# Merge blocks requested first in their slot, weight parts and constants moved in the prologue, one more float32 score tile

## The reference, cut to what matters

```python
# x: (8, 512, 512); ctx: (8, 77, 512); 16 experts, head size 64
def xattn(v, k, q, mask, W_merge, b_merge):
    scores = where(mask, -1e9, einsum('bqd,bkd->bqk', q, k) / sqrt(512))
    atted = einsum('bqk,bkd->bqd', softmax(scores), v)
    return einsum('bdl,ol->bdo', swapaxes(atted, -1, -2), W_merge) + b_merge
x = x + xattn(ctx, ctx, layernorm(x), mask, W_merge, b_merge)

h = layernorm(x).reshape(4, 1024, 512)
logits = l2norm(h) @ l2norm(sim_matrix) - sigmoid(gates)
rw = softmax over the open experts of relu(logits)       # two best ones if none is open
q, k, v = [sum over e of rw[..., e] * (h @ proj[e]) for proj in (q_proj, k_proj, v_proj)]
attn = causal softmax(q k' / 8) v
x = x + sum over e of (rw[..., e] * attn) @ o_proj[e]
```

## Time and profile before

| what | value |
|---|---|
| time before, median of 3 runs | 899.1 us (898.63 to 899.4) |
| the profiled execution, its own time | 897.96 us |
| its span | 896.2 us |
| its mean granted TensorE clock | 0.992 |
| PE busy | 871.1 us, 97% of the span |
| DVE / ACT / POOL busy | 71% / 25% / 14% |
| DMA | 96.96 MB, mean 108 GB/s |

### The profile page before, as it was taken

The page is one execution under the profiler, slowest core; times in us unless marked ns, Lnnn a source line. Parts: engine busy times, 40 slices in busy tenths (PEclk is TensorE's granted clock), DMA queues, the critical chain, the costliest instruction groups (busy, mean ns, idle before and its releaser), DMA issues.

```text
span 896.2 us, 15900 instructions
## 1 busy us (share of the span) xinstructions
PE 871.1 (97%) x4872; PEld 814.1 (91%) x4872; DVE 637.3 (71%) x1946; ACT 225.0 (25%) x567; POOL 127.2 (14%) x335
## 2 busy tenths in 40 slices
PE   6689999999999999999999999999999999999998
PEld 5689999999999999999999999999999999999996
DVE  6888868777586786767768577775767667576674
ACT  5522322213131222213212132221322112121131
POOL 5121111211011110111102011110111201011100
PEclk9799999999999999999999999999999999999999
DMA  9736415054141531425214351224415152131302
GB/s 320 288 121 167 151 51 142 27 154 129 49 132 39 164 107 61 120 59 176 84 62 120 99 166 53 86 84 130 150 38 148 35 136 92 35 98 36 97 25 94
DMA packets 68194, 96.96 MB, mean 108 GB/s; under 512 B 10905, under 2 KB 34105, under 8 KB 67874
## 3 DMA queue, kind: packets, MB, share of 16 engines
q1 hardware_dynamic: 59106, 86.79, 31.6%
q10 hardware_dynamic: 9024, 9.44, 4.5%
HBM read 77.07 MB, written 19.14 MB: 107 GB/s over the span
## 4 chain that ended last, share of the span: by engine, by line
issue 68%; PE 16%; POOLq 10%; POOL 3%; DMA 1%; DVE 1%; SPq 0%; DVEq 0%; ACT 0%; ACTq 0%
PE psQ L1328 9%; POOLq L616 2%; POOLq L596 2%; POOLq L619 2%; PE psM L1429 2%; PE psO L1429 2%; PE psQ L1429 1%; POOL limit L599 1%; POOLq L598 1%; POOLq L613 1%; POOLq L621 1%; POOL pow_out L622 1%; POOL pow_tmp L612 1%; DMA MASK<-in_mask 1%; DMA merge_lo<-merge_scratch 0%
## 5 line engine op out<-in xcount | busy, mean ns | idle before, releaser
L1328 PE MATMUL psQ<-Wqkv_hi,hT_hi 128*128 128x384 f32 (+1 forms) x1024 | 351.7, 343 | 1.8 <-DVE hT_lo L893 1.4
L1328 PE MATMUL psQ<-Wqkv_hi,hT_lo 128*128 128x384 f32 (+1 forms) x1024 | 347.3, 339 | 0.0
L1328 PE MATMUL psQ<-Wqkv_lo,hT_hi 128*128 128x384 f32 (+1 forms) x1024 | 347.2, 339 | 0.0
L1030 DVE SCALAR_TENSOR_TENSOR acc<-psQ,RW,acc 128x192 f32<-128x192 f32 x448 | 164.7, 411 | 116.5 <-PE psQ L1328 114.3
L1328 PEld LDWEIGHTS psQ<-Wqkv_hi,hT_hi 128*128 128x128 f32 x1024 | 193.7, 189 | 8.1 <-DVE hT_lo L893 1.8
L1328 PEld LDWEIGHTS psQ<-Wqkv_lo,hT_hi 128*128 128x128 f32 x1024 | 193.9, 189 | 4.6
L1328 PEld LDWEIGHTS psQ<-Wqkv_hi,hT_lo 128*128 128x128 f32 x1024 | 193.3, 189 | 0.0
L611 POOL TENSOR_TENSOR pow_tmp<-b_mv,eps 128x1 f32<-128x1 f32 x32 | 8.1, 254 | 670.5 <-DVE b_mv L983 670.5
L849 ACT ACTIVATE mixedT_hi<-spread 128x512 fp32r<-128x512 f32 x64 | 40.5, 632 | 189.2 <-DVE spread L1204 144.1
L1429 PE MATMUL psO<-Wo_hi,mixedT_hi 128*128 128x512 f32 x120 | 51.6, 430 | 0.2 <-DVE mixedT_lo L1192 0.2
L1429 PE MATMUL psO<-Wo_hi,mixedT_lo 128*128 128x512 f32 x120 | 47.2, 393 | 0.0
(11 more groups left out here) (206 smaller groups left out, 1305.3 us busy)
## 6 DMA issues: line engine op xcount, KB each, us to landing
X<-in_x SPq DMA_DIRECT2D x32, 256.0 KB, 2.7
x_scratch<-X SPq DMA_DIRECT2D x32, 256.0 KB, 2.0
spread<-gates_scratch ACTq DMA_DIRECT2D x16, 512.0 KB, 6.9
resid<-x_scratch SPq DMA_DIRECT2D x32, 256.0 KB, 4.4
out<-resid SPq DMA_DIRECT2D x32, 256.0 KB, 2.4
merge_hi<-merge_scratch SPq DMA_DIRECT2D x28, 256.0 KB, 2.9
merge_lo<-merge_scratch SPq DMA_DIRECT2D x28, 256.0 KB, 3.5
spread<-gates_scratch SPq DMA_DIRECT2D x14, 512.0 KB, 6.8
```

Of the source, the lines that this page charges most:

```text
L1030: dve.scalar_tensor_tensor(out=acc[e][:], in0=src, scalar=w, in1=acc[e][:], op0=ALU.mult, op1=ALU.add).then_inc(expert_added, 1)
L1328: last = pe.matmul(psQ[g % 4][:, 0:first_col(g) + PW], a[:, c * P:(c + 1) * P], w[:, c, E + g * PW - first_col(g):E + (g + 1) * PW], start ...
```

## The change

Six edits. `load_merge` moves to an earlier place in SP's slot, right behind the loads hung on bank turns. The tile with index 5 (the sixth) gets its context scores in float32 (`WHOLE = 6`): `turned_high` and `turned_low` drop out for it, `x1_whole_score` reads the transposed tile from `XT[1]`, and `x1_limit` takes its short form. On ACT all eight `w_high` stand in the prologue, parts 3 and 4 ahead of `copy_rows(0)`. On DVE the chain for `neg_sig` and the scaling of `sim_f` change places, `w_low(0, 0)` stands ahead of `add_x2`, `w_low(0, 1)` ahead of `normalise`, `w_low(1)` ahead of `low_rows(0)`. On POOL the power for `sim_rn` comes one turn of its loop later.

```diff
-W_AHEAD = 6
+WHOLE = 6
+        def is_whole(t1):
+            return isinstance(t1, int) and t1 < WHOLE
...
 # SP, in the slot
                             if work == "h" and cross and live(t + X1_LEAD + 1, N_TILES):
                                 load_x1(t + X1_LEAD + 1, (j + 2) % TILES, n)
+                        if qkv and k in G_AT:
+                            n = TILES * b + G_AT[k] + 1
+                            if live(n, N_TILES - TILES):
+                                load_merge(n, (G_AT[k] + 1) % TILES)
                         if prepare and g == SUM_SLOT + 1:
                             keep_x2(t + 1)
...
                             store_gates(b, GATES_T_AT[k - 1], gates_moved)
-                        if qkv and k in G_AT:
-                            n = TILES * b + G_AT[k] + 1
-                            if live(n, N_TILES - TILES):
-                                load_merge(n, (G_AT[k] + 1) % TILES)
 # POOL, prologue
-                    if n == 2:
+                    if n == TILES - 1:
                         pool.wait_ge(sim_floored, 1)
                         pool.tensor_tensor(sim_rn, sim_ss, half_e, ALU.pow).then_inc(sim_rooted, 1)
 # ACT, prologue
-                w_high(1)
-                w_high(2)
+                for g in range(1, 5):
+                    w_high(g)
                 copy_rows(0)
+                w_high(5)
+                w_high(6)
                 slice_high(1)
-                for g in range(3, W_AHEAD):
-                    w_high(g)
+                w_high(7)
 # ACT, in the slot
-                        if qkv and is_first(b) and k + W_AHEAD < PAIRS:
-                            w_high(k + W_AHEAD)
-                        if cross and g == X1_HIGH_SLOT:
+                        if cross and g == X1_HIGH_SLOT and not is_whole(t1):
                             turned_high(t1, p1)
 # DVE, prologue
                 x1_low(3, 3, 1)
+                dve.wait_ge(gate_e_made, 1)
+                link(dve.tensor_scalar(gate_e, gate_e, 1.0, None, ALU.add))
+                link(dve.reciprocal(gate_e, gate_e))
+                link(dve.tensor_scalar(neg_sig[:], gate_e, -1.0, None, ALU.mult))
+                low_ctx()
+                slice_low(0)
+                dve.wait_ge(ld_x[TILES], 32)
+                x1_moments(TILES, 0, x_first[TILES])
                 dve.wait_ge(sim_rooted, 1)
                 for c in range(KC):
                     last = dve.tensor_tensor(sim_f[:, c, :], sim_f[:, c, :], sim_rn, ALU.mult)
                 last.then_inc(sim_normed, 1)
-                low_ctx()
-                slice_low(0)
-                dve.wait_ge(ld_x[TILES], 32)
-                x1_moments(TILES, 0, x_first[TILES])
                 G_low(0)
+                w_low(0, 0)
                 x2_moved = add_x2(None)
                 row_stats(x2_moved)
-                w_low(0, 0)
                 dve.wait_ge(sim_hi, 1)
                 dve.tensor_tensor(simn[1], sim_f, simn[0].bitcast(F32), ALU.subtract).then_inc(sim_lo, 1)
+                w_low(0, 1)
                 normalise(0, 0)
-                w_low(0, 1)
+                w_low(1)
                 low_rows(0)
-                w_low(1)
-                dve.wait_ge(gate_e_made, 1)
-                link(dve.tensor_scalar(gate_e, gate_e, 1.0, None, ALU.add))
-                link(dve.reciprocal(gate_e, gate_e))
-                link(dve.tensor_scalar(neg_sig[:], gate_e, -1.0, None, ALU.mult))
                 w_low(2)
+                w_low(3)
                 slice_low(1)
-                w_low(3)
 # DVE, in the slot; x1_limit and turned_low take is_whole / WHOLE in the same way
-                        if cross and g == X1_HIGH_SLOT:
+                        if cross and g == X1_HIGH_SLOT and not is_whole(t1):
                             turned_low(t1, p1)
 # PE
                 def x1_whole_score(n):
-                    bank = next_bank(ld_xt[n], 16, has_high=False)
+                    if n < X1_LEAD:
+                        bank = next_bank(ld_xt[n], 16, has_high=False)
+                        tile = xt_first[n]
+                    else:
+                        bank = next_bank(xt_in, 16 * (n - X1_LEAD + 1), has_high=False)
+                        tile = XT[1][:]
...
                         if cross and g == X1_SCORE_SLOT:
-                            x1_score(t + X1_LEAD, (j + 1) % 2)
+                            if is_whole(t + X1_LEAD):
+                                x1_whole_score(t + X1_LEAD)
+                            else:
+                                x1_score(t + X1_LEAD, (j + 1) % 2)
```

More of the change, by code:

```diff
@@ L898, in turned_low @@
                 def turned_low(t1, p):
-                    dve.wait_ge(xt_hi, t1 - X1_LEAD + 1)
+                    dve.wait_ge(xt_hi, t1 - WHOLE + 1)
                     dve.tensor_tensor(hT[p][1][:], XT[p][:], hT[p][0][:].bitcast(F32), ALU.subtract).then_inc(xt_lo, 1)
@@ L920, in x1_limit @@
                     bank = psT[moves.bank()]
-                    if isinstance(t1, int) and t1 < X1_LEAD:
+                    if is_whole(t1):
                         dve.wait_ge(x1_scale_ready, t1 + 1)
@@ L1249, in x1_score @@
                 def x1_score(t1, p):
-                    bank = next_bank(xt_lo, t1 - X1_LEAD + 1, has_high=False)
+                    bank = next_bank(xt_lo, t1 - WHOLE + 1, has_high=False)
                     for c in range(KC):
@@ L1267, in x1_whole_score @@
                     for c in range(KC):
-                        last = pe.matmul(bank[:, 0:C], xt_first[n][:, c * P:(c + 1) * P], ctx_f[n // TILES][:, c, 0:C],
+                        last = pe.matmul(bank[:, 0:C], tile[:, c * P:(c + 1) * P], ctx_f[n // TILES][:, c, 0:C],
                                          start=(c == 0), stop=(c == KC - 1))
```

## The result

The changed kernel takes 893.03 us in the median of 6 runs (890.68 to 893.72), the one before 898.98 in the median of 6 (898.07 to 899.4). The ratio is 0.9932, with a 95% interval from 0.9919 to 0.9945: faster by 6 us or 0.7%. Forecast were 893.9 and a range from 891.3 to 896.5.

A forecast was written before the change was run, and what follows sets the result against it. TensorE bounds the kernel, waiting for merge blocks and, in the first batch, for DVE. Merge -3.8, DVE's list less the late start -2.8, clock +1.4 make -5.2: median 899.1 becomes 893.9 us, range 891.3 to 896.5.

The forecast's parts named there:

- The merge blocks: TensorE's waits for merge second halves: six of seven go with SP's earlier load, -3.8 us, bounds 2.5 and 4.2.
- the slower rival: `ctx_raw`, queued behind 512 KB of merge, lands late and ACT waits; at about 7 us landing 903.5 us; chance 0.03.
- DVE's list: First batch: 3.0 us leaves DVE's work between the first rows' split and the second tile's `normalise`; 2.8 net of late start.
- ACT's two moved parts: `w_high(3)` and `(4)` in ACT's prologue, 1.5 us each, fill 3.0 of its idle 3.75.
- The removed part of `x1_limit`: Two operations leave DVE's list in the first batch, only lengthening its 0.46 us wait for POOL's limit.
- The start: Prologue up to G comes 0.2 us late, bounds -0.3 and 0.8; inserted parts behind it have cover.
- the 0.9: `w_low(0, 1)` ahead of the first `normalise` can hold up POOL's `powers(0)`, making the start up to 0.9 us worse.
- The clock: One 2.5 us TensorE wait ahead of the second tile's transposes, then the clock falls: +1.4 us, from 0 to 1.7.
- The chances given, 0.47 to 0.25: The forecast with the clock's fall, 893.9 us, chance 0.47, against the rival without the fall, 892.5 us, chance 0.25.

The follow-up runs named there:

- e1: The kernel before with only SP's new order, `load_merge` moved earlier; 894.51 us against 898.03, 0.9964.
- e7: The changed kernel with `w_low(1)` back behind `low_rows(0)`; 893.55 us against 898.48 for the kernel before, 0.9948.
- e12: The changed kernel with 12 unread filler matmuls in TensorE's wait and the sixth tile's scores from halves; 891.56 us against 898.42 for the kernel before, 0.9922.
- e3: The changed kernel with the sixth tile's context scores made of halves again; 892.23 us against 898.03 for the kernel before, 0.9944.
- e10: The changed kernel timed again, unedited, on another run's chip; 893.16 us against 898.42 for the kernel before, 0.9944.
- e6: The changed kernel with 12 unread matmuls in TensorE's wait for the second tile's rows; 891.93 us against 898.48 for the kernel before, 0.9928.
- e4: The changed kernel with the second tile's `normalise` ahead of `x1_limit` and `w_low(7)` behind it; 890.93 us against 898.03 for the kernel before, 0.9921.
- e5: The changed kernel with the fifth tile's `x1_moments` and the scaling of `sim_f` behind `G_low(0)`; 891.71 us against 898.48 for the kernel before, 0.9930.
- e8: The changed kernel with only the scaling of `sim_f` put behind `G_low`; 892.76 us against 898.48 for the kernel before, 0.9927.
- e11: The changed kernel with 12 unread filler matmuls, timed again on the unedited changed kernel's chip; 892.04 us against 898.42 for the kernel before, 0.9926.
- e2: The changed kernel with `load_merge` back behind `store_gates`; 896.05 us against 898.03 for the kernel before, 0.9969.
- e9: The changed kernel with e4's and e5's edits together; 891.1 us against 898.42 for the kernel before, 0.9914.

## Why the prediction was right

**The merge blocks.** Forecast -3.8, bounds 2.5 and 4.2. The last piece lost 4.3 us in the profiled pair, in e1 3.9; over the twelve profiles with the new order it is 833.4 in the mean, 3.9 less than the 837.3 before. The forecast took 0.6 for each wait from the distance of starts, and 0.61 is what `sum_G` and its transpose got back in slot 21; the idle time as listed would have given 2.5 for six of them. The first batch's wait stayed, as was said. `ctx_raw`, the slower rival, never held ACT: all six of its first readers on ACT started without a wait.

**DVE's list.** Forecast 3.0 us out of it. From the first weights to the second tile's transposes were 25.17 us, and are 22.23: 2.94. (e1, with the old prologue, took 25.90, with DVE's wait of 0.66 for `w_high(3)` in it. The forecast put ACT's two moved parts only as filling idle time; that they also had to come earlier for DVE it does not say.) e7 gives one part back and finds it at full length, e12 the sixth tile's halves at 0.56 (0.68 in the forecast, of which the idle ahead of the limit gives some back: it grew from 0.46 to 0.95). The removed part of `x1_limit` did only that.

**The start.** Forecast 0.2 us late, bounds -0.3 and 0.8; in the two profiles 0.6. Over the nine profiles with this prologue (e7's differs by `w_low(1)`, but starts as the others do) the first weights come at 31.4 in the mean, with the old one (before, e1) at 30.9. 0.5 is the best figure, against two profiles only, and single ones scatter by over a microsecond. The size is inside the bounds; the place is not the forecast's. It had G late, and G was not: `G_low` starts at 22.44 in the mean of the nine and at 22.46 in the two, `sum_x2` at 23.2 in both. The time came behind it, in two parts. In four of the nine (after, e3, e10, e12) `sum_x2` ran at the low clock, 0.77 us for its first matmul instead of 0.47, and in e6 for the most part, so that the x sum came up to 2.44 us behind `G_low` instead of 1.75; in the mean of the nine that is 0.36 us, in the pair of before and after 0.69. And POOL's first power took 0.94 us instead of 0.81 behind the other half of `w_low`, which is the 0.13 that `normalise` came later behind the x sum (idle ahead of it 1.02 instead of 0.89). Whether the new prologue makes the low clock more frequent, nine profiles against two don't tell. `w_low(1)` did end in time, 0.23 of idle being left ahead of `low_rows(0)` as said (0.2).

The rule of the Trainium skill (SBUF — State Buffer, "SBUF: two separate sides"), that two SBUF inputs on VectorE shut GpSimd out for a whole instruction, would have made the start up to 0.9 us worse by the moved `w_low(0, 1)`. The trace agrees with the lock (POOL's first power for the second tile took 1.61 us behind `w_low(7)`, 0.19 without it in e4), not with the 0.9: the other half had stood in the same place before, and the difference was 0.13.

**The clock.** Forecast a wait of 2.5 us and a fall of 1.4. The wait is 2.65, the fall 26.10 - 24.81 = 1.3 (e5 and e8, with a fall, have 26.04 and 26.16, e11, without, 24.80). But it is no fixed price. Of seven profiled executions with a wait of 2.6 to 3.1 us at this place, five had a reduced clock behind it (after, e2, e5, e7, e8) and two had none (e3, e10), and e2 paid about twice. The chances given, 0.47 to 0.25, were of this kind. That the profiled execution had the fall is one of two outcomes, not a proof of the forecast's reason, that the longer wait brings it: the longest waits of the seven, 3.10 and 3.09, went one each way. The section of the Trainium skill that the prediction names for it (TensorE: Matmul & The Clock Gate, "HAM oscillation — how this bites in real kernels") tells of bursts parted by waits that are longer than nearly all of these, so it bears on the case in kind only, and the rows decide. The mean granted clock goes with the changed kernel's spread (0.994 for the fastest, 890.68, and 0.990 for those above 892), but does not explain it alone: e10 has 0.992 at 893.16 and 0.990 at 892.92.

Sum of the steps: -3.8 - 2.8 + 1.4 = -5.2, measured by pieces -4.3 - 1.65 + 0.6 = -5.3. In this pair the terms off by most are the merge part (0.5 too small) and the start (0.4 too small), and they cancel; by the means of more profiles they are 0.1 and 0.3 too small. So the mechanisms of the merge part and of DVE's list are shown, the agreement of the sums to a tenth is in part luck, and the medians moved by 5.95 us the first time and by 5.3 in e10. (The range's slow end, 899.1 less 2.5, is 896.6 and not 896.5.)

## What to carry to other kernels

In an in-order DMA queue put the load that an engine is known to wait for right behind the event that frees its buffer, and the stores and loads with slots to spare behind it; price such a wait by the distance of the starts around it, not by the idle time listed. Where an engine's list is full up to a due point, a piece of work moved out from under it was worth its whole length at that point (1.66 us in e7, 0.56 in e12), as long as its new place had cover left: in e5 and e9 it had not, and what was moved came back. Before counting on it, look whether another engine feeds the list, as ACT does here. When stalls change, look at the clock behind them: behind two waits of 0.94 and 1.43 us (e4), or 0.19 and 1.42 (e9), it stayed at 1.00; behind one of 1.74 or 1.75 it fell in both profiles that have it (before, e1), behind one of 2.6 to 3.1 in five of seven.

## What the runs showed of the hardware

- Work nobody needs made the kernel no slower: 12 matmuls of 2.95 us in TensorE's wait, granted clock 1.00 behind it in three of three profiled executions, against two of seven without them. On one chip the median was 1.1 us faster, with overlapping intervals.
- The same wait on TensorE left the clock at 1.00 in some executions and at half for some 3 us in others (0.74 and 0.92 over two stretches of 5 us are 1.7 us lost), once for about twice as long. A single profile of such a place doesn't tell which of them is usual.
- The second half of a merge block, 256 KB, landed after 3.2 us in the median and 6.7 at most in the changed kernel. The wait in the first batch's slot 19 ranged from nothing to 1.56 us over executions of nearly the same kernel. There TensorE wants the block some 5.0 us after its request. What holds that load up was not tried; ACT requests two loads of 512 KB (`spread`, 6.4 us to landing in the median) 4 to 5 us ahead of it, and from 80 to 85 us the DMA engines are full (DMA share 1.10).
- POOL was held up by DVE in three places: 0.94 us for an operation of 0.19 behind the other half of `w_low` in the prologue, 1.61 us for the same operation behind `w_low(7)`, and 2.05 us for one of 0.26 in e4.
